# The exact pass of an attention stage: units counted through eight sides, masks by GpSimd selects

## The reference, cut to what matters

```python
o1 = _attn(q, k1, v1, causal[None, None])          # branch 0: all keys up to the query
o2 = _attn(q, ks, vs)                              # branch 1: 256 selected keys, no mask
winmask = causal & (ii[:, None] - ii[None, :] < WINDOW)
o3 = _attn(q, kw, vw, winmask[None, None])         # branch 2: the last 64 keys
o = g[:, 0] * o1 + g[:, 1] * o2 + g[:, 2] * o3
return o @ Wproj
```

## Time and profile before

| what | value |
|---|---|
| median of three runs | 2942.0 us |
| the profiled execution | 2938.53 us |
| its span, first to last instruction | 2936.4 us |
| granted PE clock over the span | 0.897 |
| POOL busy in the span | 536.5 us |
| DMA, mean | 123 GB/s |

### The profile page before, as it was taken

The page is one execution under the profiler, slowest core; times in us unless marked ns, Lnnn a source line. Parts: engine busy times, 40 slices in busy tenths (PEclk is TensorE's granted clock), DMA queues, the critical chain, the costliest instruction groups (busy, mean ns, idle before and its releaser), DMA issues. The chain is left out here.

```text
span 2936.4 us, 47406 instructions
## 1 busy us (share of the span) xinstructions
PE 2361.4 (80%) x16660; PEld 1563.1 (53%) x16660; DVE 1690.2 (58%) x3159; ACT 1219.0 (42%) x2665; POOL 536.5 (18%) x575
## 2 busy tenths in 40 slices
PE   5666766665499999799999799999899999630896
PEld 3444535443365666465666465666465665320785
DVE  4754847466455664555665555665555665450676
ACT  2323423233054554354554355455355455410442
POOL 0230504215000110100110100110100110136332
PEclk9777877877699999899999899999899999855997
DMA  2361715427846556446556446556546643241113
GB/s 91 139 243 36 288 58 211 170 89 293 183 102 131 122 125 128 106 102 136 122 119 126 106 104 137 127 109 126 115 104 131 132 104 73 91 84 48 48 51 109
DMA packets 222999, 361.11 MB, mean 123 GB/s; under 512 B 68810, under 2 KB 124717, under 8 KB 222384
## 3 DMA queue, kind: packets, MB, share of 16 engines
q1 hardware_dynamic: 218448, 349.72, 47.7%
q0 software_dynamic: 4320, 8.43, 0.9%
HBM read 230.10 MB, written 126.56 MB: 121 GB/s over the span
## 5 line engine op out<-in xcount | busy, mean ns | idle before, releaser
L1342 ACT ACTIVATE prob<-ps 128x512 f32<-128x512 f32 (+5 forms) x1600 | 637.5, 441 | 740.8 <-PE ps L1293 587.5
L1395 DVE TENSOR_REDUCE maxima<-ps 128x1 f32<-128x512 f32 (+3 forms) x768 | 387.1, 547 | 299.2 <-PE ps L1224 151.2
L1314 PE MATMUL ps<-prob,plain 128*32 128x512 f32 (+5 forms) x3200 | 512.1, 443 | 0.0
L1400 DVE TENSOR_REDUCE maxima<-ps 128x2 f32<-128x512 f32 (+1 forms) x512 | 294.5, 607 | 245.0 <-PE ps L1232 98.6
L1365 POOL TENSOR_TENSOR products<-products,sums 128x256 f32<-128x256 f32 x192 | 140.7, 733 | 1611.3 <-DVE sums L1386 1610.1
L1386 DVE RECIPROCAL sums<-sums 128x256 f32<-128x256 f32 x192 | 331.5, 1736 | 104.2 <-ACT sums L1353 104.2
L1285 PE MATMUL ps<-q1a_s,k1a_s 128*128 128x512 f32 (+3 forms) x768 | 303.1, 395 | 0.0
L1293 PE MATMUL ps<-q1b_s,k1b_s 128*128 128x512 f32 (+3 forms) x768 | 301.1, 393 | 0.0
L1314 PE MATMUL ps<-prob,v_s 128*32 128x512 f32 (+3 forms) x1536 | 284.3, 491 | 0.0
L1221 PE MATMUL ps<-k1a_s,q1a_s 128*128 128x512 f32 (+3 forms) x768 | 233.3, 372 | 8.7 <-DMA k1a_s<-k1ah_dram 8.3
L1285 PEld LDWEIGHTS ps<-q1a_s,k1a_s 128*128 128x128 f32 x768 | 147.1, 192 | 126.8 <-issue 118.1
(11 more groups left out here) (329 smaller groups left out, 4774.3 us busy)
## 6 DMA issues: line engine op xcount, KB each, us to landing
qh_dram<-pairs SPq DMA_DIRECT2D x96, 512.0 KB, 3.7
kwh_dram<-pairs SPq DMA_DIRECT2D x64, 512.0 KB, 2.7
qa_s<-qh_dram SPq DMA_DIRECT2D x128, 256.0 KB, 4.5
kwa_s<-kwh_dram SPq DMA_DIRECT2D x128, 256.0 KB, 7.6
q1a_s<-qh_dram SPq DMA_DIRECT2D x128, 256.0 KB, 4.7
qb_s<-qh_dram SPq DMA_DIRECT2D x64, 256.0 KB, 9.2
kwb_s<-kwh_dram SPq DMA_DIRECT2D x64, 256.0 KB, 10.0
k1a_s<-k1ah_dram SPq DMA_DIRECT2D x32, 512.0 KB, 6.8
```

The source lines that it names most:

```text
L1314: mm = pe.matmul(ps[at:at + VD, SCORES + k % 2, q0 - c * CH:q0 - c * CH + w], w_, m.prob[:, n % PROBS, h, 0:w], start=first, stop=True, sk ...
L1342: act.activation(m.prob[:, u % PROBS, h, 0:w], ps[:, turn % SCORES, 0:w], ACT.Exp, scale=SCALE).then_inc(s["exp_done"], 1)
L1395: ins = dve.tensor_reduce(partial[:, h, i, part:part + 1], bank[:, 0:w], AX, ALU.max)
L1400: ins = dve.tensor_reduce(negs[1 if kind == "max1" else 2][:, at:at + 2], bank.rearrange("p (i n) -> p i n", i=2)[:, :, 0:w], AX, ALU.max, ...
```

## The change

It has five parts.

1. The units are counted through the eight sides (200 a block). Products come in pairs after every odd count n, for the units n - 3 and n - 2, so one unit later than before, and a side's last unit is no longer finished at the side's end. `whole` and `rows` 0 of a side come after the scores of its own unit 2. `proj` comes three units after its divisions at the soonest.
2. The mask products of the exact pass (L1288, L1291) go. POOL sets the masked probabilities to zero after the exp, by `affine_select` on both heads at once: one select for a causal unit on the diagonal, two for a window unit on it, one for the window unit that starts past it.
3. The products of a masked unit wait for the new semaphore `masked` in place of `exp_done`. POOL walks the steps of `divide` and `scores` in their order.
4. There are six buffers of probabilities in place of four.
5. The row DMAs are issued by ACT, at the step `rows`, in place of SP.

```diff
+def masked_columns(unit):
+    br, c, j, q0, w = unit
+    return int(br == 2) + int(br != 1 and q0 == j * P)
+
+def masks(side, u):
+    return side * sum(masked_columns(x) for x in UNITS) + sum(masked_columns(x) for x in UNITS[:u + 1])
-PROBS = 4
+PROBS = 6
+ROWS_AT, APART = 2, 3
...
-    return todo + [("whole", side, 0)]
-def exact_pass(w):
-def window(w, prepare):
+    return todo
...
+    total, columns = NSIDE * len(UNITS), sum(x[4] for x in UNITS)
+    steps, later = [], []
+    for n in range(total + 1):
+        w, u = divmod(n, len(UNITS))
+        if u == 0:
+            prepare, seen, at = preparation(w + 1) if w + 1 in sides else [], 0, 0
+        if n < total:
+            steps.append(("scores", w, u))
+            seen += UNITS[u][4]
+            upto = len(prepare) * seen // columns
+            steps += prepare[at:upto]
+            at = upto
+            if u == ROWS_AT and w > 0:
+                steps += [("whole", w, 0), ("rows", w, 0)]
+        ready = range(n - 3, n - 1) if n >= 3 and n % 2 == 1 else range(n - 2, n) if n == total else ()
+        for done in ready:
+            steps.append(("products",) + divmod(done, len(UNITS)))
+        for done in ready:
+            w, u = divmod(done, len(UNITS))
+            if u in LAST:
+                k = LAST.index(u)
+                steps.append(("sum", w, k))
+                if w % 2 == 1:
+                    later += [("divide", w, k, piece) for piece in range(PIECES)]
+                    if SUMS[k][0] == 0:
+                        later += APART * [None] + [("proj", w, SUMS[k][1])]
+        steps += [x for x in later[:1] if x]
+        later = later[1:]
...
-                    if br == 0 and at == 0:
-                        pe.matmul(bank[:, 0:P], m.ident_bf[:], m.causal_k[:], start=False, stop=False,
-                    if br == 2:
-                        pe.matmul(bank, m.ident_bf[:], m.window_k[:, at:at + w], start=False, stop=False,
...
-                pe.wait_ge(s["exp_done"], HP * (n + 1))
+                if masked_columns(UNITS[u]):
+                    pe.wait_ge(s["masked"], masks(side, u))
+                else:
+                    pe.wait_ge(s["exp_done"], HP * (n + 1))
...
+                if kind == "rows":
+                    act.wait_ge(s["emptied"], plan.fills.index(step) + 1)
+                    act.dma_start(dst[at:at + 1, side % 2].rearrange("p h n -> p (h n)").bitcast(F32), m.mrows[:, br, :])\
...
-            for step in plan.of(("divide",)):
+            for step in plan.of(("divide", "scores")):
+                if step[0] == "scores":
+                    if masked_columns(UNITS[u]):
+                        pool.wait_ge(s["exp_done"], HP * (n + 1))
+                    if br != 1 and at == 0:
+                        pool.affine_select(own[:, :, 0:P], own[:, :, 0:P], [[0, HP], [1, P]], ALU.is_ge, 0.0,
+                                           base=0, channel_multiplier=-1).then_inc(s["masked"], 1)
+                    if br == 2:
+                        lo = max(0, WINDOW - at)
+                        if at == 0:
+                            pool.wait_ge(s["masked"], masks(side, u) - 1)
+                        pool.affine_select(own[:, :, lo:w], own[:, :, lo:w], [[0, HP], [-1, w - lo]], ALU.is_ge, 0.0,
+                                           base=WINDOW - 1 - at - lo, channel_multiplier=1).then_inc(s["masked"], 1)
```

More of the change, by code:

```diff
@@ L1021, in block_plan @@
     sides = [k for k in range(1, NSIDE + 1) if k < NSIDE or not last]
[L1022 to L1026, removed]
+    total, columns = NSIDE * len(UNITS), sum(x[4] for x in UNITS)
[26 more added lines that the diff above has]
+        later = later[1:]
+    steps += [x for x in later if x]
+    if NSIDE in sides:
+        steps += [("whole", NSIDE, 0), ("rows", NSIDE, 0)]
     loads = [x for w in range(NSIDE) for x in (("whole", w + 1), ("local", w + 2)) if x[1] < NSIDE or not last]
     return Plan(steps, sides, loads)
-OPENING = Plan(preparation(NSIDE) + [("rows", NSIDE, 0)], [NSIDE],
+OPENING = Plan(preparation(NSIDE) + [("whole", NSIDE, 0), ("rows", NSIDE, 0)], [NSIDE],
                [("local", NSIDE), ("whole", NSIDE), ("local", NSIDE + 1)])
@@ L1165, in whole @@
                 sp.dma_start(m.v1[:, k].rearrange("p t n -> p (t n)"), src.v1).then_inc(late, 16)
[L1167 to L1173, removed]
             if cur is not None:
@@ L1183, in _ @@
                     local(side + 1)
-                for br in (2, 1, 0):
-                    row(side, br)
             if cur is not None:
@@ L1333, in _ @@
                 kind, side = step[:2]
+                if kind == "rows":
+                    br = step[2]
+                    dst, at = m.q1b if br == 0 else m.qb, ROWS[br]
+                    act.wait_ge(s["emptied"], plan.fills.index(step) + 1)
+                    act.dma_start(dst[at:at + 1, side % 2].rearrange("p h n -> p (h n)").bitcast(F32), m.mrows[:, br, :])\
+                        .then_inc(s["rows%d" % br], 16)
                 if kind == "scores":
@@ L1356, in _ @@
         def _(pool):
-            for step in plan.of(("divide",)):
+            for step in plan.of(("divide", "scores")):
+                if step[0] == "scores":
+                    _, side, u = step
+                    n = side * len(UNITS) + u
+                    br, c, j, q0, w = UNITS[u]
+                    own, at = m.prob[:, n % PROBS], q0 - j * P
+                    if masked_columns(UNITS[u]):
[9 more added lines that the diff above has]
+                                           base=WINDOW - 1 - at - lo, channel_multiplier=1).then_inc(s["masked"], 1)
+                    continue
                 _, side, k, piece = step
```

13 lines of the change are left out of this document (3 added, 10 removed).

## The result

| what | value |
|---|---|
| changed kernel | 3010.45 us, the median of 4 runs (3002.09 to 3016.28) |
| kernel before, same comparison | 2941.52 us, the median of 4 runs |
| ratio | 1.0232, interval 1.0203 to 1.0262 |
| profiled execution | 3002.09 us, span 2999.9 us |
| granted PE clock over the span | 0.886 |

The account below looks back on a forecast made before the run. PE's own work was taken to bound the attention stage. From the profiled 2938.5 us, masks off PE take 139, bursts add 6 and new waits 188: 2993.5, told as 2994 us, range 2870 to 3105.

Parts of the forecast that it names:

- (a): Odd sides: the transpose of rows 0, right behind a max2 fill, waits for `whole` on DVE, 0.95 us.
- (f): Even sides 2, 4, 6: transpose of rows 0 waits 3.0 us behind a reciprocal, masks of unit 3 another 0.5: 3.5.
- The mask term: 34 mask products a side leave PE: 4.35 us a side, 139 us over 32 sides (87 to 176).
- (b): Odd sides: after unit 6's max1 fills, the next three wait for spare banks behind DVE's reciprocals, 2.0 us.
- (c): Odd sides: burst (9, 10) waits for masks behind POOL's divisions, 3.7 us (2.6 to 6.2 by the select's cost).
- (d): Odd sides: burst (11, 12) waits behind two more divisions and the masks of 11 and 12, 0.65 us (0.3 to 3.3).
- (e): Odd sides: burst (15, 16) waits behind divisions and masks 15 and 16 after unit 12's sum, 1.8 us (1.5 to 2.5).
- rival A: New waits don't add up: time lost at (c) makes (a), (b), (d), (e) vanish; 95 us left, 2900; chance 0.27.
- the 6 for bursts: 12.5 bursts of products a side in place of 12, each costing 0.4 us beside its work: +6 us.
- The edits at nothing: Later products, six buffers, row DMAs on ACT (48 us if fully exposed), SP's loads, fewer mask constants: all taken at 0.
- B: Rival: POOL becomes the bound once a select costs over 1.7 us; at 2.36 us a select, 3329; chance 0.06.
- C: Rival: gaps in odd sides lower PE's granted clock to 0.95, 78 us more, 3072; chance 0.09.

## Why the prediction was right, and where only its sum was

**The direction, the pair and steps (a) and (f) were right.** The time is 16 us off and the pair of sides is 109.2 us against a forecast near 109 (odd 56.1 and even 53.1; the forecast's terms give 57.6 and 52.1). By the starts on the timeline, the transpose of rows 0 comes 0.99 us late in odd sides (0.95 forecast) and 2.9 in even ones (3.0). Odd sides are the longer ones, selects release late products, and PE's transposes wait for DVE. Moving `whole` alone gave back 40 us in an order otherwise the same. That confirms that (f) and (a) cost time; the forecast had 36 + 15 us for them (without (f)'s part for masks), and where the clock is 1.00 the sides give back 35, since part of the wait turns into others.

**The mask term was mis-sized: 139 us forecast, 57, 64 and 66 measured in three pairs of kernels.** Two things failed in it. First, one price was taken for masks of every width, 0.125 us for a window mask and 0.13 for a causal one, while a plain product stops getting cheaper below 192 columns and a narrow mask costs less. Odd side, PE, the scores of unit 8 (64 columns), with the banks of step (b) ahead of them:

```profile
974.22 0.28 PE L1236 MATMUL ps<-ident,maxima 128*16 128x128 f32 x1 [0.28 <-DVE maxima L1405]
974.80 1.10 PE L1218 MATMUL ps<-ksa_s,qa_s 128*128 128x256 f32 x4 [0.31 <-DVE maxima L1405]
...
975.77 0.27 PE L1272 MATMUL ps<-qb_s,kwb_s 128*128 128x64 f32 x1
975.88 0.28 PE L1271 MATMUL ps<-qa_s,kwa_s 128*128 128x64 f32 x1
```

64 columns take 0.11 us between starts, as 192 do at 980.45 to 980.56. So a mask was worth 0.13 us in causal units of 256 columns and more, 0.11 at 192, 0.07 to 0.10 at 128 and about 0.06 at 64 (medians of the same places with and without it). Summed over a side that is 3.4 to 3.6 us, 109 to 116 in all; below, 109. The Trainium skill (TensorE: Matmul & The Clock Gate, section on LDWEIGHTS) puts a weight load at its columns over 1.2 ns, so 107 ns for 128 columns as an estimate; by that rule the load and not the product would set these starts. The trace agrees in the distance, not in the length: the loads start 0.11 us apart and each has a row of 0.19 us:

```profile
980.36 0.19 PEld L1271 LDWEIGHTS ps<-qa_s,kwa_s 128*128 128x128 f32 x1
980.47 0.19 PEld L1272 LDWEIGHTS ps<-qb_s,kwb_s 128*128 128x128 f32 x1
```

Second, some of it turns into waits: without masks the kernel before gained 64 us of these 109, 1.4 us a side less. Over 1250 to 1630 us PE's scores then wait 7.6 us for exps where they waited 3.5, which is 0.6 us a side; where the other 0.8 went was not separated. The prediction's own sign for this term, a unit of 192 at about 0.48 us, came (0.45) and did not catch it: it looks at one width, and at a price where nothing waits.

**Step (c) was right in kind and half in size, (d) and (e) did not come, (b) was near.** The burst of units 9 and 10 loses 1.87 us by the starts, not 3.7; a select takes 0.41 us, not 0.6, which by the forecast's own steps makes it an estimate of 2.9. That the time PE loses earlier lets POOL catch up would explain the rest and was not tested. (b) measured 1.44 us against 2.0. (d), (e) and the masks part of (f) are 0. This is rival A, in part: of 3.7 + 0.65 + 1.8 us only 1.87 came. So the forecast of 188 us for new waits had 105 in it that the timeline shows: 0.99 + 1.44 + 1.87 = 4.3 us x 16 = 69, and 2.9 x 12 = 35.

**What stood in the place of the rest was not forecast.** The scores wait for exps behind the sum, 2.0 us in an even side and 1.6 in an odd one by PE's rows, where it was 0.4 and 0.6 before: 16 x 1.6 + 16 x 1.0 = 42 us. A fill waits 0.7 us for a bank at a later burst, 11 us in odd sides. The clock falls to half eleven times inside a side, which it never did before; ten of the sides are 1.3 to 2.6 us longer by it than the others of their kind, 17 us in all (the eleventh is the last side, which has no like). In the other direction, a wait of 0.9 us at the projection of even sides fell to 0.3, 7 us. A block's start costs nothing more: 75.1 us against 71.6 from the last odd side of a block to the next block, and 3.1 of that is what every odd side grew by. The balance is then -109 + 6 + 104 + 42 + 11 + 17 - 7 = 64 us; the profiled executions differ by 63.6. It should not close that well: the 6 for bursts is the forecast's and unmeasured, the masks are known to some 7 us, and the waits do not simply add. The 1.87 us at the burst of units 9 and 10 are 0.5 us at the side's end, against the kernel without masks. Even so, the forecast's gain was 30 us too large, its waits 84 too large, and 63 it did not have. That 2994 came within 16 us is luck: three errors of 30, 84 and 63 us cancelled. (The upper end of the forecast's own range, 3104, also joins the dearest waits with the middle price of the masks; with their bound of 87 us it would be 3155.)

**"POOL's queue" was named as the main cost, and it is not.** The forecast had 104 of its 188 us there ((c), (d), (e) and the masks' part of (f)). Without any select the new order still takes 2991 us; the selects and their queue are 19 us of the changed kernel's time. The cost is the order and what stands beside it: with the masks left on PE it takes 108 us over the kernel before. One part of it is shown by a single edit, the reciprocals of the side before ahead of `whole` (40 us). The rest lies in the places of sums and divisions, which were moved only together or with `whole` (2970 to 2934 to 2859 us).

**The edits at nothing.** The row DMAs on ACT were costed at 0, and in the changed kernel no wait of PE for a row shows between 1250 and 1630 us. But with the new order the loads on SP's queue start later in a side and the rows behind them come too late, so staying on SP would have cost 65 us. The move pays for itself and the prediction did not say so. Products a unit later and six buffers were not tried by themselves; that they cost nothing is still an argument.

**Rivals.** B fell: a select is 0.41 us against the 1.7 at which POOL would bind. The Trainium skill's figure for a body with data-dependent branching (GPSIMD Engine Reference, section on elementwise cycle accounting), an estimate of 2.6 us, does not describe this select; the trace has 0.407. C, the clock, is there in small, 17 us where C had 78: before, the clock falls to half only around the start of a block; after, it does so eleven times more, inside a side: eight stretches of 3.4 us that are worth about 1.5 us of a side's length each, and three of 6.8 us, worth 2.6 in the two sides that can be compared. The spread of 14 us between runs of the changed kernel has the size of some ten of these; that it is them was not shown.

## What to carry to other kernels

When one step of a chain is moved, follow its reader: the sum alone moved later cost 150 and 129 us; sum, reciprocals and `whole` moved together took 152 us off the changed kernel. An in-order queue charges a wait to whoever stands behind it, so for each step that can wait, list what stands behind it on the same engine. Price a removed instruction by the starts in a place where it is already absent, at the same width, and take that price as an upper end: of 109 us priced this way 64, 57 and 66 were got. When an edit moves two steps, a time inside the expected range does not say which of them did it.

## What the runs showed of the hardware

- `affine_select` on POOL, f32: 407 ns for 128x256 and 293 ns for 128x128, less than the two-input multiply of the same size at 729 ns.
- Score products of 128x128 weights in f32 start 0.11 us apart (median) at 64, 128 and 192 columns alike; 256 take 0.12, 384 0.17 and 512 0.23.
- The same gap is followed by half clock in some sides and not in others: 2.72 us at the transpose of rows 0 in five of twelve even sides of the changed kernel and in eleven of twelve without masks; 1.66 us at the burst of units 9 and 10 in six of sixteen odd sides of the changed kernel and in twelve of sixteen with `whole` early. What decides between them stays open.
